# Strided weights and reversed tokens in a float32r mixture-of-experts kernel

## The reference

```python
s0, s1, s2 = (relu(h @ share_wi[i]) @ share_wo[i] for i in range(3))      # 256 -> 1024 -> 256
out_a = relu(h @ expert_wi[type]) @ expert_wo[type]
out_b = relu(h @ expert_wi[type + 1]) @ expert_wo[type + 1]
expert_out = out_a * wa + out_b * wb
g = softmax(relu(concat(first tokens) @ gate_w1) @ gate_w2)
out = expert_out * g[0] + s0 * g[1] + s1 * g[2] + s2 * g[3]
```

## Time and profile before

| | before |
|---|---|
| median of 2 runs | 1045.24 us (1045.14 to 1045.34) |
| profiled execution, first to last instruction | 1044.1 us |
| TensorE busy | 1036.7 us (99%), 4850 matmuls |
| TensorE weight loads busy | 861.1 us (82%), 4850 loads |
| VectorE busy | 756.8 us (72%) |
| ScalarE busy | 405.0 us (39%) |
| GpSimd busy | 16.3 us (2%) |
| DMA | 223.02 MB in 38302 packets, mean 214 GB/s |
| granted TensorE clock, mean | 0.999 |

### The profile page before, as it was taken

The page is one execution under the profiler, slowest core; times in us unless marked ns, Lnnn a source line. Parts: engine busy times, 40 slices in busy tenths (PEclk is TensorE's granted clock), DMA queues, the critical chain, the costliest instruction groups (busy, mean ns, idle before and its releaser), DMA issues.

```text
span 1044.1 us, 12751 instructions
## 1 busy us (share of the span) xinstructions
PE 1036.7 (99%) x4850; PEld 861.1 (82%) x4850; DVE 756.8 (72%) x1260; ACT 405.0 (39%) x663; POOL 16.3 (2%) x26
## 2 busy tenths in 40 slices
PE   8999999999999999999999999999999999999998
PEld 5688888888888888888888888888888888888898
DVE  6989977799547986389764996559955599545236
ACT  8654555423443234422344223433334432423232
POOL 1200000000000000000000000000000000000000
PEclk9999999999999999999999999999999999999999
DMA  5388999786354754466544664546645465355582
GB/s 213 121 313 275 312 356 356 282 324 240 131 192 167 257 181 162 162 238 210 197 164 163 231 235 152 185 162 242 208 154 201 163 235 204 146 201 191 203 323 90
DMA packets 38302, 223.02 MB, mean 214 GB/s; under 512 B 4514, under 2 KB 5282, under 8 KB 16610
## 3 DMA queue, kind: packets, MB, share of 16 engines
q1 hardware_dynamic: 35938, 209.63, 56.1%
q0 software_dynamic: 2304, 12.58, 3.2%
HBM read 188.51 MB, written 33.69 MB: 213 GB/s over the span
## 4 chain that ended last, share of the span: by engine, by line
PE 96%; DMA 2%; DVE 2%; issue 0%; SPq 0%; ACT 0%; DVEq 0%
PE ps_up L665 14%; PE ps_up L695 14%; PE ps_up L696 14%; PE ps_down L737 14%; PE ps_down L741 14%; PE ps_down L738 14%; PE ps_aux L658 2%; PE ps_aux L659 2%; PE ps_aux L660 2%; DMA wi<-split_wi 1%; DVE y L1633 1%; PE ps_aux L837 1%; PE ps_aux L834 1%; PE ps_aux L833 1%; PE ps_aux L822 1%; PE ps_aux L818 1%
## 5 line engine op out<-in xcount | busy, mean ns | idle before, releaser
L1065 ACT ACTIVATE hid_hi<-ps_up 128x512 fp32r<-128x512 f32 (+1 forms) x336 | 193.5, 576 | 507.8 <-PE ps_up L665 507.6
L1306 DVE SCALAR_TENSOR_TENSOR hid_lo<-ps_up,hid_hi 128x512 fp32r<-128x512 f32 (+1 forms) x336 | 220.1, 658 | 228.9 <-ACT hid_hi L1065 227.5
L695 PE MATMUL ps_up<-x_hi_all,wi 128*128 128x512 f32 (+1 forms) x660 | 250.8, 382 | 0.4 <-DMA wi<-split_wi 0.4
L696 PE MATMUL ps_up<-x_hi_all,wi 128*128 128x512 f32 (+1 forms) x660 | 249.9, 380 | 0.0
L737 PE MATMUL ps_down<-hid_hi,wo 128*128 128x512 f32 (+1 forms) x640 | 245.3, 384 | 0.1
L738 PE MATMUL ps_down<-hid_hi,wo 128*128 128x512 f32 (+1 forms) x640 | 245.1, 384 | 0.0
L665 PE MATMUL ps_up<-x_lo_all,wi 128*128 128x512 f32 (+1 forms) x660 | 197.4, 380 | 0.2 <-DVE x_lo_all L1297 0.2
L741 PE MATMUL ps_down<-hid_lo,wo 128*128 128x512 f32 (+1 forms) x640 | 193.9, 384 | 0.0
L695 PEld LDWEIGHTS ps_up<-x_hi_all,wi 128*128 128x128 f32 x660 | 124.1, 188 | 24.1 <-DMA wi<-split_wi 0.8
L696 PEld LDWEIGHTS ps_up<-x_hi_all,wi 128*128 128x128 f32 x660 | 124.1, 188 | 23.0
L665 PEld LDWEIGHTS ps_up<-x_lo_all,wi 128*128 128x128 f32 x660 | 122.0, 188 | 24.3 <-DVE x_lo_all L1297 0.4
(11 more groups left out here) (248 smaller groups left out, 855.1 us busy)
## 6 DMA issues: line engine op xcount, KB each, us to landing
wi<-split_wi SPq DMA_DIRECT2D x70, 1024.0 KB, 4.8
wo<-split_wo SPq DMA_DIRECT2D x70, 1024.0 KB, 4.9
modb<-mod_scratch SPq DMA_DIRECT2D x28, 512.0 KB, 4.6
split_wi<-wi SPq DMA_DIRECT2D x10, 1024.0 KB, 7.3
split_wo<-wo SPq DMA_DIRECT2D x10, 1024.0 KB, 7.6
xt<-in_x SPq DMA_DIRECT2D x8, 512.0 KB, 5.8
split_wi<-ex POOLq DMA_DIRECT2D x4, 1024.0 KB, 8.6
split_wo<-ex POOLq DMA_DIRECT2D x4, 1024.0 KB, 6.0
```

The source lines that it names most:

```text
L695: pe.matmul(ps, w_hi, x2_hi[:, parity, c, tokens], start=c == 0, stop=False)
L696: pe.matmul(ps, w_lo, x2_hi[:, parity, c, tokens], start=False, stop=False)
L1065: act.activation(hid_hi[:, k % NU, tokens], ps_up[k % NU][:, tokens], ACT.Relu).then_inc(hid_hi_ready, 1)
L1306: dve.scalar_tensor_tensor(hid_lo[:, k % NU, tokens], ps_up[k % NU][:, tokens], 0.0, f32(hid_hi[:, k % NU, tokens]), ALU.max, ALU.subtract ...
```

## The change

In four parts, all of them about where and in which order TensorE reads SBUF:

- The weights are laid out on the host so that the columns of two neighbouring blocks of 128 alternate (`paired`). `column_block` reads one of them with a step of two: even block numbers from the pair's first element, odd ones from its second.
- The tokens are read backwards by the up matmuls (x2_hi, x2_lo), so ps_up and hid hold them in reversed order, and backwards again by the down matmuls (hid_hi, hid_lo), which puts them right. In the opening, where `up` is done in two halves, a half goes to the other half of the bank (`mirrored`).
- Each high and low tile of wi gets 32 unused elements behind it and each of wo 16. The DMAs between them and DRAM now have two pieces a partition, of 1,024 elements each.
- EDGE goes from 128 to 96, which makes room for the pads.

```diff
-EDGE = 128
+EDGE = 96
+WI_PAD = 32
+WO_PAD = 16
+def back(tokens):
+    return slice(tokens.stop - 1, tokens.start - 1 if tokens.start else None, -1)
+def column_block(at):
+    start = at // (2 * P) * 2 * P + at // P % 2
+    return slice(start, start + 2 * P - 1, 2)
...
-        wi = sb("wi", [P, 2, 2, CT * UF], F32R)
-        wo = sb("wo", [P, 2, 2, UT * E], F32R)
+        wi = sb("wi", [P, 2, 2, CT * UF + WI_PAD], F32R)[:, :, :, 0:CT * UF]
+        wo = sb("wo", [P, 2, 2, UT * E + WO_PAD], F32R)[:, :, :, 0:UT * E]
...
+        def mirrored(tokens):
+            return slice(T - tokens.stop, T - tokens.start)
...
-                sp.dma_start(f32(wi[:, buf, :, :]).rearrange("p s f -> p (s f)"), source).then_inc(wi_landed[buf], 16)
+                sp.dma_start(f32(wi[:, buf, :, :]), source.rearrange("p (s f) -> p s f", s=2)).then_inc(wi_landed[buf], 16)
...
-                    mm = pe.matmul(ps, w_hi[c], x2_lo[:, parity, c, tokens], start=False, stop=c == CT - 1)
+                    mm = pe.matmul(ps, w_hi[c], x2_lo[:, parity, c, back(tokens)], start=False, stop=c == CT - 1)
...
-                ps = ps_up[at % NU][:, tokens]
+                ps = ps_up[at % NU][:, mirrored(tokens) if opens else tokens]
...
-                        return [w[:, c, j * P:(j + 1) * P] for w in again_wi[u % 2]]
-                    cols = slice(c * UF + j * P, c * UF + (j + 1) * P)
+                        return [w[:, c, column_block(j * P)] for w in again_wi[u % 2]]
+                    cols = column_block(c * UF + j * P)
...
-                    pe.matmul(ps, w_hi, x2_hi[:, parity, c, tokens], start=c == 0, stop=False)
-                    pe.matmul(ps, w_lo, x2_hi[:, parity, c, tokens], start=False, stop=False)
+                    pe.matmul(ps, w_hi, x2_hi[:, parity, c, back(tokens)], start=c == 0, stop=False)
+                    pe.matmul(ps, w_lo, x2_hi[:, parity, c, back(tokens)], start=False, stop=False)
...
-                    cols = slice(j * E + c * P, j * E + (c + 1) * P)
+                    cols = column_block(j * E + c * P)
...
-                    pe.matmul(bank, w_hi[:, cols], hid_hi[:, at % NU, tokens], start=start, stop=False)
-                    pe.matmul(bank, w_lo[:, cols], hid_hi[:, at % NU, tokens], start=False, stop=False)
+                    pe.matmul(bank, w_hi[:, cols], hid_hi[:, at % NU, back(tokens)], start=start, stop=False)
+                    pe.matmul(bank, w_lo[:, cols], hid_hi[:, at % NU, back(tokens)], start=False, stop=False)
...
-                    mm = pe.matmul(bank, w, hid_lo[:, at % NU, tokens], start=False, stop=stop)
+                    mm = pe.matmul(bank, w, hid_lo[:, at % NU, back(tokens)], start=False, stop=stop)
...
+    def paired(w):
+        return w.reshape(*w.shape[:-1], -1, 2, P).swapaxes(-1, -2).reshape(w.shape)
```

More of the change, by code:

```diff
@@ L507, in keep_wi @@
                 sp.wait_ge(wi_ready, u + 1)
-                sp.dma_start(kept_place(split_wi, u), f32(wi[:, u % 2, :, :]).rearrange("p s f -> p (s f)"))\
+                sp.dma_start(kept_place(split_wi, u).rearrange("p (s f) -> p s f", s=2), f32(wi[:, u % 2, :, :]))\
                     .then_inc(wi_kept[u % 2], 16)
@@ L513, in keep_wo @@
                 sp.wait_ge(wo_ready, u + 1)
-                sp.dma_start(kept_place(split_wo, u), f32(wo[:, u % 2, :, :]).rearrange("p s f -> p (s f)"))\
+                sp.dma_start(kept_place(split_wo, u).rearrange("p (s f) -> p s f", s=2), f32(wo[:, u % 2, :, :]))\
                     .then_inc(wo_kept[u % 2], 16)
@@ L543, in load_wo @@
                 sp.wait_ge(down_done, (count - 1) * UT)
-                sp.dma_start(f32(wo[:, buf, :, :]).rearrange("p s f -> p (s f)"), source).then_inc(wo_landed[buf], 16)
+                sp.dma_start(f32(wo[:, buf, :, :]), source.rearrange("p (s f) -> p s f", s=2)).then_inc(wo_landed[buf], 16)
             def load_again_wi(half):
@@ L729, in down @@
                         pe.wait_ge(hid_ready, b * SLOTS + (at + 1))
-                        pe.matmul(banks[0][0], banks[0][1], hid_lo[:, at % NU, tokens], start=False, stop=True)\
+                        pe.matmul(banks[0][0], banks[0][1], hid_lo[:, at % NU, back(tokens)], start=False, stop=True)\
                             .then_inc(last_down, 1)
@@ L1013, in opening @@
                 for k in range(LAG):
-                    up_rest(ps_up[k][:, half(0)], [wi_hi[:, 0, c * UF + k * P:c * UF + (k + 1) * P] for c in range(CT)], 0, half(0))
+                    up_rest(ps_up[k][:, half(1)], [wi_hi[:, 0, column_block(c * UF + k * P)] for c in range(CT)], 0, half(0))
                 open_turn_back(1)
@@ L1830 @@
         every(a["L1_cond_gate_vecs"])], axis=1)
+    def paired(w):
+        return w.reshape(*w.shape[:-1], -1, 2, P).swapaxes(-1, -2).reshape(w.shape)
     def wi_units(w):
-        return w.reshape(-1, CT, P, 2, UF).transpose(0, 3, 2, 1, 4).reshape(-1, 2, P, CT * UF)
+        return paired(w.reshape(-1, CT, P, 2, UF).transpose(0, 3, 2, 1, 4).reshape(-1, 2, P, CT * UF))
     def wo_units(w):
-        return w.reshape(-1, 2, UT, P, E).transpose(0, 1, 3, 2, 4).reshape(-1, 2, P, UT * E)
+        return paired(w.reshape(-1, 2, UT, P, E).transpose(0, 1, 3, 2, 4).reshape(-1, 2, P, UT * E))
     sent = {
```

## The result

| | before | after |
|---|---|---|
| median | 1045.24 us | 1069.59 us (1069.47 to 1069.70) |
| ratio | | 1.0235, 95% interval 1.0205 to 1.0264 |
| profiled execution | 1044.1 us | 1067.8 us |

The account below looks back on a forecast made before the run. The prediction took TensorE to be the bound, time being a number of matmuls times their spacing. It summed 1045.2 us before, minus 40 for relieved matmuls, plus 2 for DMAs, to 1007 us, with a range of 999 to 1060 us.

Parts of the forecast that it names:

- The 13.3 ns: Each float32r matmul's time beyond its columns at 2.4 GHz: 226.7 ns against 213.3 for 512 columns.
- rival 1: Up and down matmuls: the surcharge is a fixed float32r weight-change cost, so 1045 us, or 1047 with DMAs; chance 0.18.
- Readers in step pay either nothing or always, by their distance: SBUF reads by weight load and backward tokens: a constant distance, set by the pads, could remove 10.9 ns per matmul.
- the term of -40 us: 4,044 up and down matmuls: 10.9 ns less each is 44 us, with one in ten counted as not relieved.
- the case 0.55: Up and down matmuls: most pairs relieved, giving 1007 us, own range 999 to 1023; chance 0.55.
- Readers that cross pay the same whatever their start: SBUF reads before the change: load and tokens cross repeatedly, giving the uniform 227 ns whatever the tiles' addresses.
- a surcharge that doubles, 54 us: Up and down matmuls: a load spanning twice the bytes doubles the surcharge, 13.3 ns x 4,044 = 54 us slower.
- rival 3: Up and down matmuls: the step-of-two load costs 26.7 ns instead of 13.3, 1099 us, or 1142 at half pace; chance 0.15.
- A load with a step of two isn't slower in itself: Weight loads: two hits per 16-byte SBUF line suffice for full bandwidth, so a possible 97 us loss falls away.
- The DMAs cost about 2 us: Two-piece 1 MB split-weight transfers: mostly hidden, 2 us for thin cover at 60 to 200 us and around 212 us.
- 44 us are there to be gained: Best end for 4,044 up and down matmuls: spacing falls from 226.7 to 215.8 ns, giving 1001 us.
- The context matmuls stay at 227: Context stage: matmuls with unchanged operands should keep 227 ns, telling the mechanism from a change of the whole engine.

Follow-up runs that it names:

- tokens_one: Kernel before, but the moving operand of the up and down matmuls is one token read 512 times; 1019.64 us, ratio 0.9754.
- tokens_twice: Kernel before, but the up and down matmuls read each of the first half of their tokens twice in a row; 1020.52 us, ratio 0.9766.
- weights_one_column: Kernel before, but each weight load of the up and down matmuls reads one column 128 times; 1057.52 us, ratio 1.0117.
- stride_back: Kernel before with weights read at a step of two and tokens read backwards, no pads; 1070.89 us, ratio 1.0253.
- pads_64b: Kernel before with pads of 64 bytes in both wi and wo and edge 96; 1063.13 us, ratio 1.0176.
- pads_only: Kernel before with only the change's pads (128 bytes in wi, 64 in wo) and its edge of 96; 1061.46 us, ratio 1.0166.
- shift_only: Kernel before with edge 96 and an unused tile behind wo, high and low tiles keeping their distance; 1045.81 us, ratio 1.0008.
- pads_256: Kernel before with pads of 256 bytes in both wi and wo and edge 16; 1046.76 us, ratio 1.0018.
- tokens_one_stride: Kernel before with weights read at a step of two, no pads, and one token read 512 times as moving operand; 1022.83 us, ratio 0.9789.
- stride_only: Kernel before with only the weights interleaved and read at a step of two, tokens forward, no pads; 1067.92 us, ratio 1.0220.
- tokens_by_two: Kernel before, but the up and down matmuls read the even tokens of their 512, then the odd ones; 1908.09 us, ratio 1.8259.

## Why the prediction was wrong

- **TensorE is the bound; time is a count by a spacing.** Right: the up and down matmuls give 22.9 us by their mean step and the context matmuls 1.1, of 24.35.
- **The 13.3 ns hold a quarrel of two readers in SBUF.** Half shown. I inferred it from the plain float32 matmuls and the earlier trace rows; tokens_one and tokens_twice show that 11 ns go with the tokens' walk, with 215 to 220 and 215.8 ns, so rival 1, a fixed cost, falls. That the load's reading has a part in these 11 ns is not shown, and weights_one_column speaks against it. What the load's step adds to them does need both readers: 6.7 ns with walking tokens, nothing with still ones. There the Trainium skill's rule that TensorE's two read ports are independent and that it never waits on anyone (SBUF — State Buffer, Who interferes with whom) does not hold.
- **"Readers in step pay either nothing or always, by their distance, and the pads are what sets the distance."** This is the step that failed: the term of -40 us, a relief of 10.9 ns for nine matmuls in ten. None was relieved; the spacing of the 512-wide ones rose by 6.7 ns, some 24 us in sum, and that of the 256-wide ones stayed. In the kernel after, the high and low tiles of wi differ by 128 bytes in their distance from the tokens and the four tiles of wo stand at 0, 64, 128 and 192 bytes, taken by 256; all of them run at 233 to 234 ns, and stride_back, with no pads, does the same. None of these distances was the good one. I had taken the direction of the load from no row, and said so, but still gave the case 0.55. Whether the load walks up or down stays open; weights read backwards weren't tried.
- **"Readers that cross pay the same whatever their start, which is what the uniform 227 shows."** Wrong reading of a right row. The uniform step was a rhythm that settles, and it depends on the distances: pads_64b and pads_only change nothing else that shift_only and pads_256 don't clear, and pay 17 to 18 us. The kernel before stood at the better of the steady states seen with tokens walking at full pace, and each part of the change leaves it.
- **One part's bound: a surcharge that doubles, 54 us.** The sign of rival 3 was right and its size too large: the surcharge rose from 32 to 48 clocks, not to 64. I gave the whole slower side 0.15 and ended the range at 1060, 10 us short. Half of rival 3 (27 us, 1072) was the case to have priced, and three edits of an access pattern that had settled should have had more than 0.15 between them.
- **A load with a step of two isn't slower in itself.** Nearly right. At 512 columns it costs nothing with still tokens (tokens_one_stride), at 256 columns 6 ns. The record grew by 5 to 9 ns, and a longer record did not mean a slower kernel.
- **The DMAs cost about 2 us.** Right in size: at most 1.5 us in pads_256, and no new wait in the kernel after. The 8 KB pieces did become 4 KB ones.
- **44 us are there to be gained.** Wrong, by what I had not put on the sum: I took VectorE, busy 81% of its fullest stretch, to have room enough. tokens_twice shows 24 us.
- **The context matmuls stay at 227.** Nearly: L833 to L838 with ct have medians of 227; those with xg run at 229 to 232 in the mean. One cause is xg's edge of 96 elements, by which its second channel tile lies 128 bytes off a multiple of 256 from the first: in shift_only, which has this edge and neither pads, step nor backward tokens, those with xg run at 229 to 231 and those with ct at 227, and in stride_only, with the edge of 128, the medians of both are 227. It isn't the only one, as stride_back with the edge of 128 has 228 to 231 for both.

What stays open: why the steady states are 226.7 and 233.3 ns and nothing between, why both together are hardly worse than one, why a load of one column is at some 231, and whether the 11 ns of the kernel before need the load at all. No version was found that beats the kernel before and makes its products.

## What to carry to other kernels

When TensorE is bound by matmuls in float32r with a weight load each, look at the start-to-start time against the columns at the clock: what is above 2.5 ns may come from how the tokens and the weights are read, and then the layout of SBUF is part of the time. Keep tiles that are read in turn at distances of whole multiples of 256 bytes and read both operands in rising order without a step; a pad of 64 or 128 bytes cost 1.7% here without adding any work. Before pricing a relief, try it with the moving operand held still: that run bounds what can be gained, and shows who is the next bound. Holding the weights still gave no such bound here.

## What the runs showed that I had not expected

- A moving operand in float32r with a step of two comes at half rate: 451 ns for 512 columns (tokens_by_two) against 226.7.
- A weight load with a step of two costs nothing by itself at 512 columns and 6 ns at 256 (tokens_one_stride against tokens_one); one with a step of four makes 256-wide matmuls take 233 ns instead of 120.
- Pads of 64 or 128 bytes between weight tiles cost 17 to 18 us, of 256 and 512 bytes 1 to 2 us.
- Step of two and backward tokens each take the matmul from 226.7 to 233.3 ns, and both together hardly further.
- With tokens at half the pace of addresses the surcharge of a matmul falls from 13.3 to 2.5 ns.
